# Two cross-attention stages: a batch's side jobs laid out anew over its twelve slots

## The reference

```python
q = (x @ Wq.T + bq).reshape(B, NQ, 16, 16)
k = (context @ Wk.T + bk).reshape(B, NKV, 16, 16)
v = (context @ Wv.T + bv).reshape(B, NKV, 16, 16)
attn = softmax(einsum('bihd,bjhd->bhij', q, k) * SCALE, axis=-1)
out = einsum('bhij,bjhd->bihd', attn, v).reshape(B, NQ, 256)
return out @ Wo.T + bo
```

## Time and profile before

| | before |
|---|---|
| median of 3 runs | 4155.93 us (4153.95 to 4162.15) |
| profiled execution | 4163.89 us, span 4162.1 us |
| mean granted TensorE clock | 0.864 |
| PE / PEld busy | 3100.2 us (74%) / 2412.7 us (58%) |
| DVE busy | 1736.9 us (42%) |
| ACT busy | 1238.4 us (30%) |
| POOL busy | 847.2 us (20%) |

### The profile page before, as it was taken

One profiled execution on the slowest core, in us unless ns is written; L12 is line 12 of the kernel. 1 busy time (PEld: TensorE's weight loads), 2 busy tenths in 40 slices (PEclk: granted clock), 3 DMA queues, 4 the chain that ended last, 5 costly groups with the idle time before them and its releaser, 6 DMA issues. The chain is left out here.

```text
span 4162.1 us, 59447 instructions
## 1 busy us (share of the span) xinstructions
PE 3100.2 (74%) x19704; PEld 2412.7 (58%) x19704; DVE 1736.9 (42%) x3457; ACT 1238.4 (30%) x2520; POOL 847.2 (20%) x934
## 2 busy tenths in 40 slices
PE   1888884788888896049999438868888888836990
PEld 1565653566666665038888425546666666625870
DVE  2333336565555565110000234446666666622332
ACT  0222224344444442013333112224444444401220
POOL 0000000333222331500000320013332233232005
PEclk8778785899999996569999769979999999958995
DMA  3000000000000002445565310000000000014653
GB/s 101 0 0 0 0 0 0 12 12 13 12 12 12 12 12 92 124 137 185 185 190 194 110 30 0 0 11 12 13 12 12 12 10 12 4 56 157 202 185 107
DMA packets 174511, 234.54 MB, mean 56 GB/s; under 512 B 25136, under 2 KB 141328, under 8 KB 174336
## 3 DMA queue, kind: packets, MB, share of 16 engines
q1 hardware_dynamic: 156448, 184.23, 14.3%
q0 software_dynamic: 17888, 47.73, 3.5%
HBM read 186.04 MB, written 45.88 MB: 56 GB/s over the span
## 5 line engine op out<-in xcount | busy, mean ns | idle before, releaser
L1188 DVE TENSOR_REDUCE x_neg_max<-banks 112x2 f32<-112x750 f32 x512 | 479.3, 937 | 456.6 <-PE banks L924 454.1
L1119 POOL TENSOR_TENSOR x_qH<-x_q_high,head_mask 128x448 fp32r<-128x448 f32 x256 | 260.5, 1018 | 1930.1 <-DVE x_q_low L1176 1930.1
L1068 ACT ACTIVATE x_probT<-banks 125x448 f32<-125x448 f32 x768 | 417.4, 544 | 537.9 <-PE banks L944 525.1
L940 PE MATMUL banks<-x_qH,x_kS 128*125 128x448 f32 x768 | 379.1, 494 | 70.8 <-issue 44.0
L1629 PE MATMUL banks<-f_xT,f_w 128*128 128x256 f32 x1680 | 386.3, 385 | 15.2 <-DMA f_w<-in_L_ffn_w 10.4
L1641 PE MATMUL banks<-f_w,f_hT 128*128 128x256 f32 x1680 | 374.2, 379 | 0.0
L1629 PEld LDWEIGHTS banks<-f_xT,f_w 128*128 128x128 f32 x1680 | 319.7, 192 | 74.0 <-issue 21.3
L1641 PEld LDWEIGHTS banks<-f_w,f_hT 128*128 128x128 f32 x1680 | 313.9, 190 | 39.9
L944 PE MATMUL banks<-x_diag,x_ones 112*125 112x448 f32 x768 | 284.7, 371 | 0.0
L942 PE MATMUL banks<-x_qL,x_kS 128*125 128x448 f32 x768 | 283.9, 370 | 0.0
L924 PE MATMUL banks<-x_kS,x_qH 128*112 128x376 f32 x1024 | 265.4, 340 | 7.3 <-issue 7.3
(11 more groups left out here) (269 smaller groups left out, 4928.1 us busy)
## 6 DMA issues: line engine op xcount, KB each, us to landing
f_w<-in_L_ffn_w SPq DMA_DIRECT2D x70, 1024.0 KB, 8.3
f_w<-in_L_ffn_w SPq DMA_DIRECT2D x70, 512.0 KB, 4.4
f_x_slots<-slot_x SPq DMA_DIRECT2D x70, 256.0 KB
slot_y<-f_y POOLq DMA_DIRECT2D x70, 256.0 KB, 5.1
f_ctx_rows<-in_ctx SPq DMA_DIRECT2D x32, 281.2 KB
x_cnat<-in_ctx SPq DMA_DIRECT2D x32, 281.2 KB
slot_x<-f_zero SPq DMA_DIRECT2D x10, 896.0 KB, 11.6
x_ctxT<-in_ctx_T SPq DMA_DIRECT2D x32, 187.5 KB
```

The lines of the kernel that those rows point to most:

```text
L940: pe.matmul(to, kS[:, r, q, keys], qH[:, r, heads, :].rearrange("p h t -> p (h t)"), start=True, stop=False)
L1068: act.activation(probT[:, u % 2, c].rearrange("k h t -> k (h t)"), ST[i % 2][0:KB, 0:HU * T], ACT.Exp).then_inc(exp_done, 1)
L1119: pool.tensor_tensor(qH[:, r, to, :], wide(q_high[:, q:q + 1, :], 1, HU), mask, ALU.mult).then_inc(qH_ready, 1)
L1188: dve.tensor_reduce(mx[:, u % 2, 2 * pair:2 * pair + 2], psum[0:T, 2 * pair:2 * pair + 2, 0:NKV], AX_X, ALU.max, negate=True).then_inc(max ...
```

## The change

The table `AT` is rewritten. In slots (1 to 11; slot 0 has no job in either):

| slot | 1 | 2 | 3 | 4 | 5 | 6 | 7 | 8 | 9 | 10 | 11 |
|---|---|---|---|---|---|---|---|---|---|---|---|
| layer 0 before | xT | q | k0 | k1 | back | v01 | v2 | oT | y | | |
| layer 0 after | xT | q | k0 | | back | k1 | | v01 | v2 | oT | y |
| layer 1 before | cT0 | cT1 | xT | q | back | k0 | k1 | v01 | v2 | | |
| layer 1 after | xT | q | cT0 | cT1 | k0 | | back | k1 | | v01 | v2 |

DVE makes the low halves of `k0` and `k1` (`LATE`) in the slot behind the job's, after that slot's `neg_max` and `make_diag`. `norm_x` runs ahead of slot 0's `neg_max` and not behind it; `norm_context` moves from slot 0 to slot 2. The waits on `JOB` follow the new neighbours. Cut to its core:

```diff
-        AT = {"xT": 1, "q": 2, "k0": 3, "k1": 4, "back": 5, "v01": 6, "v2": 7, "oT": 8, "y": 9}
+        AT = {"xT": 1, "q": 2, "k0": 3, "back": 5, "k1": 6, "v01": 8, "v2": 9, "oT": 10, "y": 11}
...
-        AT = {"cT0": 1, "cT1": 2, "xT": 3, "q": 4, "back": 5, "k0": 6, "k1": 7, "v01": 8, "v2": 9}
+        AT = {"xT": 1, "q": 2, "cT0": 3, "cT1": 4, "k0": 5, "back": 7, "k1": 8, "v01": 10, "v2": 11}
...
+    LATE = ("k0", "k1")
...
                         if k == 0:
                             pe.wait_ge(cn_ready, ONE + b + 1)
-                            pe.wait_ge(v2_ready, ONE + b)
+                            pe.wait_ge(q_ready, ONE + b + 1)
...
                         pe.wait_ge(xn_ready, ONE + b + 1)
-                        if layer == 1:
-                            pe.wait_ge(cT1_ready, ONE + b + 1)
-                        else:
-                            pe.wait_ge(v2_ready, ONE + b)
+                        pe.wait_ge(v2_ready, ONE + b)
+                        if layer == 0:
                             pe.wait_ge(x_done, ONE + since(g, GROUP, s - 2))
...
                         m = 0 if j == "k0" else 1
-                        if m == 0:
+                        if m == 0 and layer == 0:
                             pe.wait_ge(q_ready, ONE + b + 1)
-                            if layer == 0:
-                                pe.wait_ge(ctx_loaded[r], g * (16 * GROUP) + 32 * (s // 2 + 1))
-                            else:
-                                pe.wait_ge(o_ready, ONE + since(g, GROUP, s - 1))
-                        else:
+                            pe.wait_ge(ctx_loaded[r], g * (16 * GROUP) + 32 * (s // 2 + 1))
+                        if m == 0 and layer == 1:
+                            pe.wait_ge(cT1_ready, ONE + b + 1)
+                        if m == 1:
                             pe.wait_ge(kS_low, ONE + g * (SU * GROUP) + SU * s + 2)
+                            pe.wait_ge(o_ready, ONE + since(g, GROUP, s - 1))
...
                             pe.wait_ge(kS_low, ONE + g * (SU * GROUP) + SU * (s + 1))
-                            if layer == 0:
-                                pe.wait_ge(o_ready, ONE + since(g, GROUP, s - 1))
...
                     pe.wait_ge(o4_ready, ONE + g * NU + SU * (s + 1))
-                    if layer == 0:
+                    if made_next:
+                        pe.wait_ge(kS_low, ONE + since(g, SU * GROUP, SU * (s + 2) + 2))
+                    elif layer == 0:
                         pe.wait_ge(x_done, ONE + since(g, GROUP, s))
-                        if made_next:
-                            pe.wait_ge(kS_low, ONE + since(g, SU * GROUP, SU * (s + 3)))
                     else:
                         pe.wait_ge(o_ready, ONE + since(g, GROUP, s))
-                        if made_next:
-                            pe.wait_ge(q_ready, ONE + since(g, GROUP, s + 3))
...
+                        if at == 0 and more:
+                            norm_x(g, s + 1)
                         if c < 2 and (u + 1 < NU or not last):
                             neg_max(g, u + 1, c)
                             if c == 1:
                                 make_diag(g, u + 1)
-                        if at == 0 and more:
-                            if layer == 1:
-                                norm_context(g, s + 1)
-                            norm_x(g, s + 1)
+                        if layer == 1 and at == 2 and more:
+                            norm_context(g, s + 1)
                         j = SLOT.get(at)
-                        if j in MAKE and more:
+                        if SLOT.get(at - 1) in LATE and more:
+                            copies(g, s + 1, SLOT[at - 1])
+                        if j in MAKE and j not in LATE and more:
                             copies(g, s + 1, j)
```

## The result

| | before | after |
|---|---|---|
| median of 4 runs | 4154.94 us (4151.76 to 4162.15) | 4197.57 us (4194.81 to 4201.04) |
| profiled execution, its span | 4163.89, 4162.1 us | 4198.82, 4197.0 us |
| layer 0, 31 batches from `xT` to `xT` | 813.7 us | 859.5 us |
| the same in layer 1 | 834.6 us | 834.6 us |
| layer 0, mean of 20 common batches | 25.59 us | 27.13 us |

The change makes the kernel slower: ratio 1.0101, interval 1.0083 to 1.0118. A common batch is one of the 20 that neither hold a turn of the group loop, nor come first, nor follow a turn. All of the loss is in layer 0. Layer 0 lost 45.8 us and layer 1 nothing; the medians differ by 42.6, the two profiled spans by only 34.9. In the stretch between the two layers, where nothing is changed, the profiled execution after took 1180.4 us, 21 less than before (1201.7; 1195 to 1205 in every other trace here).

The account below looks back on a forecast made before the run. PE, busy in 74% of the span, was taken to bound the kernel, so stalls were summed: layer 0 +5.3, layer 1 -12.7, turns +7.5, making 0 us; 4156 us against the median of 4155.93, range 4132 to 4186.

Parts of the forecast that it names:

- the clock rival: PE's clock falls behind the new stalls, some 1.3 us for each of two in 62 batches: +160 us, 4316; chance 0.02.
- The chains: PE waits while DVE makes late low halves: layer 0 `back` 1.86 us, `v01` 1.69; layer 1 1.40 at each.
- the 0.11: DVE's step from `diag` to the low halves: a gap instead of an overlap adds 0.11 us in three places, +10 us.
- Layer 1: Layer 1's batches: stalls sum to 3.34 us in place of 3.76; with restart and `q`, -0.41 us a batch.
- The stalls that go: PE's old waits vanish: layer 0 0.79, 0.58, 1.14 and 0.69 us; layer 1's diag wait 0.72 and `cT0` 1.10.
- What is late next: Whatever follows a key job waits for low halves made a slot later; layer 0's stalls sum to 3.66 us, not 3.31.
- The turns: At the group loop's 5 turns in each layer, 0.6 and 0.9 us more than a common batch: +7.5 us.
- The rival that ends slower: In layer 0's slot 4 a POOL product catches `diag` for most of its 0.93 us: +29 us, 4185; chance 0.21.

Follow-up runs that it names:

- the one-fold filling: The changed kernel with one needless matmul ahead of the waits of `back` and of `v01` in layer 0; 4170.59 us, ratio 1.0009 to the kernel before.
- the version with another order: The changed kernel with the late low halves made ahead of `make_diag` in layer 0; 4193.64 us, ratio 1.0050 to the kernel before.
- `back` filled: The changed kernel with three needless matmuls ahead of the wait of `back` only, in layer 0; 4186.94 us, ratio 1.0042 to the kernel before.

## Why the prediction was wrong

**The step that failed** is the weight of the clock rival: "PE is busy up to each stall, so little speaks for it", chance 0.02. The comparison drawn for it was the right one, 0.73 behind the 3.03 of a turn and 0.47 behind the 0.79 of slot 0; but the new stalls of 1.9 lie between these two, and none of the rows read told on which side. A stall longer than any seen inside a batch was an unknown with bounds of no falls and a fall at each, and 0 was taken for it. Measured: 22 falls in 61 stalls, 1.4 us each (1.3 was taken), 21 of them within the 31 batches, 29 of the 45.8 us that layer 0 lost. The price of the rival, 160 us, was also wrong, since it let layer 1's stalls of 1.5 fall too, and every stall of layer 0: all of layer 1's and two thirds of layer 0's keep the clock.

The trace of before had more to say. At the start of layer 1 the same instruction stands on both sides of a stall of 1.94 us (layer 0 starts with one as long, the 1.9 of the earlier trace rows):

```profile
2761.53 1.53 PE L896 MATMUL banks<-x_ctxT,x_wk 128*128 128x375 f32 x4 [0.72 <-DVE x_q_all L1169]
2764.99 2.87 PE L896 MATMUL banks<-x_ctxT,x_wk 128*128 128x375 f32 x4 [1.94 <-DVE x_kS L1181]
```

PE had idled several times just before, so this isn't the case asked about, but here a stall of this length lost the clock. On the other side, of the five turns of layer 0, which idled 3.0 to 3.4 us, only two lost it (3.44 and 3.03) and three kept it (3.03 to 3.21). Neither length nor the row at 3.03 alone decides, and why a given stall falls stays open.

**The chains** were right in mechanism and a little short. Their common part was an overlap of 0.08 ahead of the low halves; it is a gap of 0.03. Layer 0, in the batch shown: `back` 1.90 for 1.86 (`diag` took 0.73, not 0.80, which gives back 0.07 of the 0.11), `v01` 1.80 for 1.69. Over all batches this `diag` took 0.78 and `back` idled 1.89, which is 1.96 from start to start. A batch with its clock takes 26.10 (the one-fold filling) and not 25.59 + 0.17: 0.51 x 31 = 16 us, the other part of the 45.8. Of the 0.34 that the forecast lacked, 0.2 is in these chains, 0.10 in `y`, which behind values holds PE for 0.77 us and not for 0.67 (priced for `q` in layer 1 only); the last 0.04 was not traced.

**Layer 1** was to gain 0.41 a batch and gained 0.06. `back` and `v01` are 0.09 and 0.10 longer by that gap. `k1` stalls 0.85 for 0.54, because slot 7's `diag` took 0.94 and not the 0.64 assumed: POOL's addition ran beside it. I had weighed that clash for layer 0, where it cost what was taken, and not for layer 1, where it took 0.3 x 31 = 9 us. With these terms the batch should have lost 0.09 and not gained 0.06; the 0.15 between them was not traced.

**The stalls that go** went, all of them: no `x_diag`, no `x_xn`, no `x_cnat` releases PE in a batch. The version with the low halves in their own slot shows what that is worth alone, 2.0 us a batch. "What is late next" was named rightly too. What I never asked is whether the lateness is needed: the empty slot alone already gives DVE its time.

**The turns** were to cost 0.6 and 0.9 us more each. At the five turns of layer 0 PE now idles 1.99 to 2.43, 2.18 on average, and not 3.03 to 3.44, 3.15 on average:

```profile
988.58 0.73 PE L937 MATMUL banks<-x_qH,x_kS 128*125 128x448 f32 x1 [2.43 <-issue]
```

The modelled end of `y` makes this idling look shorter. From the start of values to the next exponent a turn took 3.93 on average before and takes 4.01 now, with the 0.67 of `y` in it; so about 0.6 of `y` is hidden there, where 0.5 was taken. Over turn and next batch layer 1 took 0.5 us more than before, layer 0 3.1, of which 1.0 is the chains' (2 x 0.51) and the rest the 7 falls outside the common batches. The turns move by more than this between kernels that are the same there, so the term as a whole is neither shown nor refuted.

**Added up**, over a forecast of 0 for the two layers: 29 us of falls, 31 x 0.34 = 10.5 in layer 0's batches and 31 x 0.35 = 11 in layer 1's make 50.5. Measured are 45.8; the turns and the first batches gave the rest back.

**The rival that ends slower**, POOL catching `diag` in slot 4, was wrong for this kernel (0.71 to 0.85, 0.78 on average), and true of the version with another order.

## What to carry over

Before a job is moved so that PE waits once for long where it waited several times briefly, ask whether the trace shows a stall of that length with the clock kept; if it doesn't, both outcomes belong in the sum. An empty slot behind a job and a later reader are two cures for one stall: try the slot alone first. And wherever a `diag`-like product on DVE joins a chain that PE waits for, look at what POOL does in that very microsecond, in each place of the program.

## What was not expected of the hardware

- Idling of 1.6 to 2.0 us at a stretch, with PE busy up to it, lowered the clock in 22 of 61 cases, for some 3.4 us, costing 1.4 us each; 1.9 at `back` more often (18 of 30) than 1.7 at `v01` (10 of 31 with `back` filled). Idling of 3.1 to 3.3 lowered it in 58 of 62 (the kernel with late low halves alone). Idling of 1.1 to 1.3 lowered it in none, but 0.99 and 0.91 with 0.6 us of work between them did so in 13 of 21 such pairs, in the version with the low halves ahead of `diag`. Adding matmuls that nobody needs made the stage 21 to 36 us shorter (some 15 of the 36 at the turns and in the first batch).
- The same layer-1 instructions took 28.9 to 32.0 us in the batch with the loop's turn: 31.0 to 32.0 in three kernels on one chip, 28.9 to 29.7 in three on another. Whether the program around them or the chip makes the difference isn't shown. Over the five turns of the layer it is 15 us, 0.4%, more than many a change to be measured.
